# A two-layer graph kernel whose set-up is dealt out anew: squares and a chunk of unit rows on ScalarE, a first part of x of half size, transposes behind the third scores, first block weighed four pairs behind

## The reference

```python
def _L0_gnn_ref(x, adj, beta):                       # attention over the neighbours
    norm2 = jnp.linalg.norm(x, axis=1, keepdims=True)
    cos = beta[0] * (x @ x.T) / (norm2 @ norm2.T + 1e-07)
    masked = cos + (1.0 - adj) * -1000000000.0
    P = jax.nn.softmax(masked, axis=1)
    return P @ x

def _L1_gnn_ref(x, edge_index, weight):
    return jnp.matmul(edge_index, jnp.matmul(x, weight))

x = _layernorm(x + _L0_gnn_ref(x, adj, L0_gnn_beta), axis=-1)     # x 4096 x 128 f32
x = _layernorm(x + _L1_gnn_ref(x, adj, L1_gnn_weight), axis=-1)   # adj 4096 x 4096 f32 of 0 and 1
```

## Time and profile before

| | before |
|---|---|
| median of 3 runs | 496.63 us (495.28 to 497.84) |
| profiled execution, its time | 496.09 us |
| span of that execution | 494.3 us |
| PE busy | 465.7 us (94%) |
| DVE busy | 379.5 us (77%) |
| ACT busy | 312.8 us (63%) |
| POOL busy | 52.5 us (11%) |

### The profile page before, as it was taken

The page is one execution under the profiler, slowest core; times in us unless marked ns, Lnnn a source line. Parts: engine busy times, 40 slices in busy tenths (PEclk is TensorE's granted clock), DMA queues, the critical chain, the costliest instruction groups (busy, mean ns, idle before and its releaser), DMA issues.

```text
span 494.3 us, 8871 instructions
## 1 busy us (share of the span) xinstructions
PE 465.7 (94%) x3491; PEld 302.8 (61%) x3491; DVE 379.5 (77%) x637; ACT 312.8 (63%) x358; POOL 52.5 (11%) x64
## 2 busy tenths in 40 slices
PE   0769999999999999999999999999989999999994
PEld 0436676676676676666676766767764455555484
DVE  5979999999999999999999999999973022211253
ACT  4759888898898889889878988987861000000000
POOL 4400000210020020001002002000100000000011
PEclk9989999999999999999999999999999999999998
DMA  7999999999999999998996998970042010011111
GB/s 201 97 110 121 113 114 129 118 148 158 116 146 111 158 146 120 148 139 73 149 141 93 132 136 129 85 148 21 1 172 77 9 39 26 21 44 42 44 42 44
DMA packets 101690, 50.20 MB, mean 102 GB/s; under 512 B 69376, under 2 KB 98208, under 8 KB 101664
## 3 DMA queue, kind: packets, MB, share of 16 engines
q0 software_dynamic: 17952, 16.78, 41.1%
q1 hardware_dynamic: 83424, 33.05, 32.0%
q10 hardware_dynamic: 288, 0.07, 0.1%
HBM read 77.40 MB, written 22.82 MB: 203 GB/s over the span
## 4 chain that ended last, share of the span: by engine, by line
PE 78%; DVE 9%; DMA 4%; ACT 3%; issue 3%; POOL 1%; POOLq 0%; ACTq 0%; DVEq 0%
PE psum L944 22%; PE psum L888 20%; PE psum L892 10%; PE psum L865 9%; PE psum L867 9%; PE psum L866 9%; DVE E L641 4%; ACT E L424 2%; DVE el L649 2%; DMA adjT<-adj_bytes 2%; PE psum L954 1%; DMA adj_bytes<-in_adj 1%; DMA adjT<-in_x 1%; DVE xaug L726 1%; POOL rn L367 1%
## 5 line engine op out<-in xcount | busy, mean ns | idle before, releaser
L888 PE MATMUL psum<-xaug,eh 128*128 128x257 f16 x1024 | 185.9, 275 | 7.8 <-DVE uT L538 4.7
L424 ACT ACTIVATE E<-psum,sc 128x1024 f32<-128x1024 f32 x128 | 154.1, 1204 | 51.7 <-PE psum L867 50.8
L892 PE MATMUL psum<-xaug,el 128*128 128x129 f16 x1024 | 176.7, 222 | 0.0
L641 DVE SCALAR_TENSOR_TENSOR E<-E,adjT 128x1024 f32<-128x1024 f32 x128 | 156.0, 1219 | 14.4 <-ACT E L424 11.8
L649 DVE SCALAR_TENSOR_TENSOR el<-E,eh 128x1024 f16<-128x1024 f32 x128 | 155.8, 1217 | 0.0
L433 ACT ACTIVATE eh<-E 128x1024 f16<-128x1024 f32 x128 | 133.9, 1046 | 1.7 <-DVE E L641 1.7
L888 PEld LDWEIGHTS psum<-xaug,eh 128*128 128x128 f16 x1024 | 99.7, 98 | 36.8 <-DVE uT L538 5.2
L944 PE MATMUL psum<-adjT,uT 128*128 128x512 fp8e4 (+1 forms) x576 | 112.1, 355 | 0.0
L892 PEld LDWEIGHTS psum<-xaug,el 128*128 128x128 f16 x1024 | 100.8, 98 | 13.3
L865 PE MATMUL psum<-uT 128*128 (+1 forms) x256 | 97.9, 382 | 0.0
L866 PE MATMUL psum<-uT 128*128 (+1 forms) x256 | 97.5, 381 | 0.0
(11 more groups left out here) (71 smaller groups left out, 156.7 us busy)
## 6 DMA issues: line engine op xcount, KB each, us to landing
adj_bytes<-in_adj POOLq DMA_DIRECT2D x31, 512.0 KB, 12.4
adjT<-in_x SPq DMA_DIRECT2D x4, 512.0 KB, 6.9
xres<-in_x SPq DMA_DIRECT2D x8, 256.0 KB, 3.5
q_row<-norms SPq DMA_DIRECT2D x8, 256.0 KB, 8.5
x_rows<-x SPq DMA_DIRECT2D x8, 256.0 KB, 2.9
E<-x_rows SPq DMA_DIRECT2D x8, 256.0 KB, 3.0
out<-E SPq DMA_DIRECT2D x16, 128.0 KB, 2.2
x_parts<-x1p SPq DMA_DIRECT2D x7, 256.0 KB, 7.7
```

The costliest lines, as they stand in the source:

```text
L424: nc.scalar.activation(E[:, m % RING, :, :], S[m % 2], ACT.Exp, bias=col(C_BB), scale=col(C_BS)).then_inc(e_done, 1)
L641: nc.vector.scalar_tensor_tensor(out=e, in0=e, scalar=EPRE, in1=mask_bytes(b, m), op0=ALU.mult, op1=ALU.min).then_inc(masked, 1)
L888: return nc.tensor.matmul(O[t][:, 0:XC], eh[:, s, a, cols], xaug[:, j, :], start=start, stop=stop)
L892: return nc.tensor.matmul(O[t][:, 0:D + 1], el[:, s, a, cols], xaug[:, j, 0:D + 1], start=False, stop=False)
```

## The change

In the order of the set-up:

- **Squares.** Of chunk 0 ACT now sums three tiles (before none), of the others four as before; DVE sums 5, 4, 4 and 4 tiles (`SQ_V`) where it summed 8, 4, 4 and 4. DVE's `unit_rows(0)` stands ahead of the squares of chunk 2.
- **Unit rows.** Chunk 1 is made by ACT in eight instructions of one tile each (`unit_rows_a`), which it reads from a scaled copy `rn_a` of the norms. DVE makes chunks 0, 2 and 3.
- **Masks.** `FIRST` is four slices of one pair. The cast of slice 0 is issued when the first chunk of x has landed, ahead of the first power; cast 2 waits for slice 3.
- **xres.** Its load stands behind the transposes of block 0 on SP.
- **Transposes.** Group 2 is turned behind the scores of pair 0, group 3 behind those of pair 1, groups 4 to 7 behind those of pair 2. The norms are turned through bank 7 in place of bank 4.
- **x parts.** `xaug` is written in five parts, of 4, 4, 8, 8 and 8 tiles (`XPART`), at pairs 0, 2, 4, 7 and 10.
- **Lag.** In block 0 the weighing is four pairs behind the scores (`LAG0`), and after the last scores of the block there is one weighing more, so that block 1 begins three behind as before.

```diff
-    FIRST = [(0, 1), (1, 1), (2, 2)]
+    FIRST = [(0, 1), (1, 1), (2, 1), (3, 1)]
+    XPART = [(0, 4), (4, 8), (8, 16), (16, 24), (24, 32)]
...
-        XAUG_AT = (0, 4, 7, 10)
+        XAUG_AT = (0, 2, 4, 7, 10)
+        LAG0 = LAG + 1
+        SQ_V = (5, 4, 4, 4)
...
-            sp.dma_start(rows_in_twos(xres[:, :, :]), x_v[0]).then_inc(xres_in, 16)
...
             load_mask(0)
+            sp.dma_start(rows_in_twos(xres[:, :, :]), x_v[0]).then_inc(xres_in, 16)
...
+            pool.wait_ge(x_in[0], 16)
+            cast_first(0)
             inverse_norms(0)
-            cast_first(0)
             cast_first(1)
+            cast_first(2)
             inverse_norms(1)
-            cast_first(2)
+            cast_first(3)
...
+            def unit_rows_a(c):
+                act.wait_ge(rn_done, c + 1)
+                nc.scalar.activation(rn_a[:, :], rn[:, chunk(c)], ACT.Copy, scale=USC).then_inc(rn_scaled, 1)
+                act.wait_ge(rn_scaled, 1)
+                for t in range(CT):
+                    last = nc.scalar.activation(work[:, c * CT + t, :], xfull[:, c * CT + t, :], ACT.Copy,
+                                                scale=rn_a[:, t:t + 1])
+                last.then_inc(u_done_a, 1)
+
             uT_hi_part(0)
+            unit_rows_a(1)
             uT_hi_part(1)
...
             for m in range(NP):
+                if m == 2:
+                    for g in range(4, UG):
+                        uT_hi_part(g)
                 exp_pair(0, m)
+                if m < 2:
+                    uT_hi_part(m + 2)
                 if m in XAUG_AT:
                     xaug_hi(XAUG_AT.index(m))
-                if m == 1:
-                    split_hi(0, 0)
-                if m < LAG:
-                    uT_hi_part(2 * m + 2)
-                    uT_hi_part(2 * m + 3)
-                if m > 1:
+                if m > 0:
                     split_hi(0, m - 1)
...
+            def weigh_first(m):
+                for c, (t, _) in enumerate(XPART):
+                    if t == 2 * m:
+                        pe.wait_ge(x_lo, c + 1)
+                weigh(m, m)
...
-                if m == LAG:
+                if m == LAG0:
                     pe.wait_ge(uT_lo, UG)
-                if m >= LAG:
-                    if (m - LAG) % (CT // 2) == 0:
-                        pe.wait_ge(x_lo, (m - LAG) // (CT // 2) + 1)
-                    weigh_lagged(0, m)
+                if m >= LAG0:
+                    weigh_first(m - LAG0)
+            weigh_first(NP - LAG0)
```

More of the change, by code:

```diff
@@ L74, in resnorm_graph_kernel @@
         rn = sb("rn", [P, NT], F32)
+        rn_a = sb("rn_a", [P, CT], F32)
         q = sb("q", [P, NT], F32)
@@ L399, in _ @@
             act.dma_start(w_sb[:, :], weight).then_inc(w_in, 16)
-            for c in range(1, NC):
+            for c in range(NC):
                 act.wait_ge(x_in[c], 16)
-                for t in range(c * CT + CT // 2, (c + 1) * CT):
+                for t in range(c * CT + SQ_V[c], (c + 1) * CT):
                     last = nc.scalar.activation(work[:, t, :], xfull[:, t, :], ACT.Square, accum_out=n2[:, t:t + 1])
@@ L436, in xaug_hi @@
             def xaug_hi(c):
+                ts = slice(*XPART[c])
                 act.wait_ge(xs_step, 5)
-                nc.scalar.activation(xaug[:, chunk(c), 0:D], xfull[:, chunk(c), :], ACT.Copy,
-                                     scale=col(C_XS)).then_inc(x_hi, 1)
+                nc.scalar.activation(xaug[:, ts, 0:D], xfull[:, ts, :], ACT.Copy, scale=col(C_XS)).then_inc(x_hi, 1)
             def read_out(b):
@@ L517, in sum_squares @@
                 dve.wait_ge(x_in[c], 16)
-                for t in range(c * CT, c * CT + (CT if c == 0 else CT // 2)):
+                for t in range(c * CT, c * CT + SQ_V[c]):
                     last = nc.vector.tensor_tensor_reduce(out=work[:, t, :], in0=xfull[:, t, :], in1=xfull[:, t, :],
@@ L633, in mask_pair @@
                 dve.wait_ge(e_done, n + 1)
-                if not later(b) and m < 3:
+                if not later(b) and m < len(FIRST):
                     dve.wait_ge(first_in[m], 16)
@@ L724, in xaug_lo @@
             def xaug_lo(c):
+                ts = slice(*XPART[c])
                 dve.wait_ge(x_hi, c + 1)
-                nc.vector.scalar_tensor_tensor(out=xaug[:, chunk(c), D + 1:XC], in0=xfull[:, chunk(c), :],
-                                               scalar=col(C_XS), in1=xaug[:, chunk(c), 0:D], op0=ALU.mult,
-                                               op1=ALU.subtract).then_inc(x_lo, 1)
+                nc.vector.scalar_tensor_tensor(out=xaug[:, ts, D + 1:XC], in0=xfull[:, ts, :], scalar=col(C_XS),
+                                               in1=xaug[:, ts, 0:D], op0=ALU.mult, op1=ALU.subtract).then_inc(x_lo, 1)
             def layer(tiny):
@@ L738, in layer @@
                         move_norms()
[L739 to L743 removed]
+                    if m == 0:
+                        uT_lo_part(2)
                     if m in XAUG_AT:
                         xaug_lo(XAUG_AT.index(m))
[L746 removed]
+                    if m == 1:
+                        uT_lo_part(3)
+                    if m > 0:
                         split_lo(0, m - 1)
+                    if m == 1:
+                        for g in range(4, UG):
+                            uT_lo_part(g)
                 def block_of_rows(b):
```

45 lines of the change are left out of this document (23 added, 22 removed).

## The result

| | before | changed |
|---|---|---|
| median of 20 runs | 496.76 us (495.25 to 497.93) | 495.07 us (493.42 to 496.69) |
| ratio to before | 1 | 0.997, 95% interval 0.9959 to 0.998 |
| span of the profiled execution | 494.3 us | 493.3 us |

The changed kernel is 1.5 us faster, 1.0 to 2.0 by the interval. The forecast was 3.2: the direction was right, the size double.

What follows compares the result with a forecast made beforehand. The attention runs at PE's pace, but late masks limit the gain: the least of 3.8, 3.6, 3.2 and 5.0 is 3.2 us. 496.09 - 3.2 = 492.9 profiled, 493.4 with the median 0.5 above; range 491.6 to 495.9.

Steps and rivals of the forecast that it cites:

- The set-up: Before the first weighing: pair 0's mask at about 18.8 in place of 20.23, first weighing at 27.6 in place of 31.00.
- piece 1: Mask stream: lands at 34.0, 1.5 us earlier; pair 4's mask comes 2.7 earlier and the end 3.8.
- Piece 2: Mask stream: two closed DMA holes and the moved xres sum to 2.55 us; lands at 45.9, the end 3.6 earlier.
- xres: Load moved behind block 0's transposes: 0.75 us gained ahead of Piece 2, 0.75 added ahead of Piece 4.
- Piece 4: Mask stream: 20.0 us behind Piece 2 plus 0.75 for xres, so 1.8 earlier; the end 3.2 earlier, the smallest limit.
- The tolerance of DVE in block 1: Around pair 16: DVE may be somewhat late there, counted as 1.25 us of the 3.2 gain.
- The lag: Block 0, weighing four pairs behind: where DVE or a mask is late, the end gains a further 1.1 us.
- PE's own limit: PE alone, from its earlier first weighing and scores done ahead, could end 3.4 + 1.3 + 0.3 = 5.0 us earlier.
- Rival 1: Mask stream: masks do not move, the early cast delays x; only the lag's 1.1 to 1.3 us remain: 495.4, chance 0.22.
- Rival 2: Set-up: the slices' transposes queue one behind the other, slice 3 landing at 32.6: 499.6, chance 0.07.
- Rival 3: PE: its clock falls again in stops at pairs 4 and 8, taking 5.0 down to 2.0: 494.6, chance 0.10.
- Rival 4: Mask stream: pieces 1, 2 and 4 come as early as DVE wants, gain held by PE to 5.0: 491.6, chance 0.07.

Runs made afterwards that it cites:

- e17: Changed kernel with a light mask stream, casts 1 to 5 replaced by byte copies (result not the reference's): 490.36 us, 0.9886 of the kernel before.
- e5: The changed kernel measured and profiled a second time, nothing altered: 494.71 us, 0.9967 of the kernel before.
- e14: The changed kernel measured and profiled a third time, nothing altered: 494.52 us, 0.9965 of the kernel before.
- e16: Changed kernel with cast 1 held until slice 3 has landed: 499.24 us in one run.
- e1: Changed kernel with cast 2 issued when slice 1 has landed, no longer slice 3: 494.44 us, 0.9969 of the kernel before.
- e7: Changed kernel with xres loaded right behind x, as before the change: 492.96 us, 0.9939 of the kernel before.
- e9: Changed kernel with xres loaded right behind x, second measurement: 0.9944 of the kernel before.
- e15: Changed kernel with xres loaded right behind x, third measurement: 493.35 us, 0.9949 of the kernel before.
- e4: Changed kernel with block 0's weighing three pairs behind the scores in place of four: 495.74 us, 0.9991 of the kernel before.

## Why the prediction was wrong, step by step

- **The set-up was right.** First power forecast at 7.3, found at 7.54; last slice cast 12.1 and 12.18; unit rows on ACT 0.30 each, found 2.44 us for eight; mask of pair 0 at 18.8 and 18.81; first weighing at 27.6 and 27.70. DVE was ready for pair 4 at 32.3 by the forecast (its terms, 18.8 + 13.7, add up to 32.5), at 32.0 by its last row in front of it. ACT's timeline, the eight unit rows:

```profile
12.61 2.44 ACT L434 ACTIVATE adjT<-adjT,rn_a 128x128 f32<-128x128 f32 x8
```

- **Masks as the limit: right** (e17). So was the form of the sum, the least of several limits with the one of piece 4 the smallest, and **piece 1**: 34.0 forecast, pair 4's mask at 33.90, though the other two profiles (cast 3 at 34.38 and 36.15) say that this fit was partly luck.
- **Piece 2: the step that failed.** The sum had 0.9 + 0.9 + 0.75 = 2.55 us from two holes and xres; the profile had 0.85 (cast 4 at 47.66 against 48.51; 48.94 and 46.66 in e5 and e14). The first hole closed. The second needed slice 3 by 25, for which I had reckoned 22 to 24 by its size; it landed at 25.9, since here the slice's transposes beside cast 1 ended only with it (e16: 2.6 us with no cast of a piece beside them, 8.2 beside). The hole moved to 25 to 27 and grew. Nor is a hole's length a gain: with that hole filled in e1 piece 2 came 11 us earlier and the ratio did not move.
- **xres: wrong.** Counted as 0.75 us gained ahead of piece 2 and as much lost ahead of piece 4, so as nothing in the smallest term, its move costs 1.2 us (e7, e9, e15 against the changed kernel). Without it the gain is 2.8, so this alone is most of the distance between 3.2 and 1.5; why it costs that is open.
- **Piece 4.** Cast 6 was forecast at 66.7, 1.8 us earlier, and found at 68.22, 0.3 earlier (68.65 and 67.33 in e5 and e14). It followed from piece 2: 20.56 us behind cast 4, 20.75 forecast with xres in it. Of the 2.2 us by which the profiled time missed its forecast (495.08 against 492.9) this is 1.5; the rest is the next point and the 0.3 us lost in block 3, for which the sum had no term. This does not add to the point on xres: that load acts through these landings.
- **The tolerance of DVE in block 1: 1.25 forecast, 0.73 found.** The mask of pair 16 came 0.57 earlier (0.3 from the landing and 0.27 that DVE had to spare, where 0.1 was counted), the weighing of pair 16 1.30. I had looked for the narrowest low half (pair 24). The first thing that PE wants of DVE in block 1 is the reading out of block 0, for which it idles 0.77 where it idled 0.2 before; that stands earlier. In e5, e9 and e15, where piece 2 sets the end, PE idles 0.2 there as before.
- **The lag: right.** 1.1 forecast; e4 1.1 by the ratios, 1.2 in its rows at its own casts.
- **PE's own limit: 5.0 forecast, 6.1 found** (e17). What I had left out is the clock: the first pair of weighing and scores took 35.10 - 31.00 = 4.1 us before, with the granted clock at 0.66, and takes 30.36 - 27.70 = 2.66 now, with 1.00. The long idling in front of it is gone (4.74 us before, 1.06 now).
- **The rivals.** Rival 1 (masks do not move, 1.1 to 1.3 us) has the size nearest to the result. Its mechanism is not shown: x's chunks landed nearly when they did before (ACT's first squares of chunks 1 and 2, which wait for x, start at 7.79 and 9.29, 7.71 and 9.23 before; chunk 3 is not waited for), so the early cast took at most 0.1 us from x, and the hole at 10 to 12 closed. The rule of the Trainium skill (DMA: Bandwidth & Descriptors, section Queues, rings and completion order), by which an engine takes its queues in turn, was cited beside this rival; a delay of x from one cast beside it is not to be seen in this trace. Rival 2 did not come (slice 3 landed at 25.9, not past 29.6), but was nearer to the mechanism: not one slice behind the other, but the slice beside the cast. Rival 3, the clock falling again in the new stops, did not come in the changed kernel's first profile (1.00 behind stops of 1.72 and 1.55 us) but did in e5, a profile of the same kernel, behind a stop of 3.20 us:

```profile
40.00:45.00 5.00, 5.00 (x35) 3.44 (x33) 5.00 (x5) 4.32 (x5) 0.00 (x0) 0.69 1.16 108
```

It cost nothing at the end there, since "pair 16" stands where piece 2 puts it (48.94 + 27.1 = 76.04, found 76.03). So the argument against it, that a stop of less than half of 4.74 us would not do, does not hold in general (e15: 2.17 us). Rival 4 (masks as early as DVE wants them) needs what only the light stream of e17 gives.

## What to carry to other kernels

When two engines are relieved and a stream of transfers feeds them, read the stream as a ladder (who is released by whom) and sum the rungs; the holes in the DMA share are not a budget. A transfer's duration in a trace is its duration beside what ran with it: before a short one is counted at its size, ask what is queued beside it. And a load moved "out of the way" has to be measured alone. When two landings take turns in setting the end, a profile shows one draw of them: note for each which one it was before explaining a difference.
